# Scores of two 64-node graphs as 64 by 64 products in the two halves of the partitions, in place of masked 128 by 128 products

## The reference, cut to what matters

```python
h = relu(layernorm(x))
q, k, v = h @ Wq.T, h @ Wk.T, h @ Wv.T            # float32
rel = einsum('bnd,bmd->bnm', q, k) * adj.T         # 64 x 64 for each set
rel = rel / norm(rel, axis=2)
x = x + einsum('bnm,bmd->bnd', rel, v)
h = relu(layernorm(x))
for _ in range(3):                                 # w3, w4, w5, u3, u5: 256-wide layers
    a = adj @ h                                    # both halves of the input are the same
    z = sigmoid(a, h);  r = sigmoid(a, h);  c = tanh(a, r * h)
    h = (1 - z) * h + z * c
x = x + h
```

## Time and profile before

| | |
|---|---|
| median of three runs | 916.28 us (915.57 to 917.47) |
| the profiled execution | 915.86 us |
| its span, first to last instruction | 914.1 us |
| granted TensorE clock, mean | 0.996 of full speed |
| instructions | 14622 |
| busy | PE 98%, weight load 85%, DVE 83%, ACT 57%, GpSimd 12% |
| DMA | 98.73 MB, mean 108 GB/s |

### The profile page before, as it was taken

The page is one execution under the profiler, slowest core; times in us unless marked ns, Lnnn a source line. Parts: engine busy times, 40 slices in busy tenths (PEclk is TensorE's granted clock), DMA queues, the critical chain, the costliest instruction groups (busy, mean ns, idle before and its releaser), DMA issues.

```text
span 914.1 us, 14622 instructions
## 1 busy us (share of the span) xinstructions
PE 899.9 (98%) x4760; PEld 772.9 (85%) x4760; DVE 754.1 (83%) x1513; ACT 520.9 (57%) x892; POOL 107.8 (12%) x161
## 2 busy tenths in 40 slices
PE   8999999999999999999999999999999999999996
PEld 7878888888888888888888888888888888888885
DVE  5877879889788887888978888888879888797665
ACT  5465664656457574665745656456655556555552
POOL 1210102101021010210101101120101201020000
PEclk9999999999999999999999999999999999999999
DMA  6013222623245142441414513154221632224222
GB/s 180 24 50 113 93 93 94 205 69 110 84 125 186 46 138 86 143 161 46 147 60 138 184 69 115 46 163 158 91 92 53 204 110 92 92 102 129 73 66 92
DMA packets 75394, 98.73 MB, mean 108 GB/s; under 512 B 8176, under 2 KB 65776, under 8 KB 75376
## 3 DMA queue, kind: packets, MB, share of 16 engines
q1 hardware_dynamic: 75376, 98.50, 33.0%
HBM read 50.76 MB, written 47.71 MB: 108 GB/s over the span
## 4 chain that ended last, share of the span: by engine, by line
PE 95%; DVE 2%; issue 1%; DMA 1%; ACT 1%; SPq 0%; DVEq 0%
PE gate L410 14%; PE gate L411 14%; PE gate L412 14%; PE cand L412 9%; PE cand L410 9%; PE cand L411 9%; PE fea L552 9%; PE fea L485 3%; PE tok L410 3%; PE tok L411 2%; PE tok L412 2%; PE fea L410 1%; PE fea L412 1%; PE fea L411 1%; DMA x_s<-x 1%
## 5 line engine op out<-in xcount | busy, mean ns | idle before, releaser
L796 ACT ACTIVATE r_s<-gate,b_r 128x512 f32<-128x512 f32 x96 | 65.7, 690 | 126.5 <-PE gate L412 126.5
L1110 DVE TENSOR_TENSOR rh<-r_s,h 128x512 f32<-128x512 f32 x96 | 68.5, 745 | 31.1 <-ACT r_s L796 30.6
L809 ACT ACTIVATE z_s<-gate,b_z 128x512 f32<-128x512 f32 x96 | 64.1, 683 | 51.5 <-PE gate L412 51.5
L712 ACT ACTIVATE h_hi<-h 128x512 fp32r<-128x512 f32 x92 | 56.8, 628 | 39.9 <-DVE h L909 21.9
L1082 DVE SCALAR_TENSOR_TENSOR d_s<-z_s,h 128x512 f32<-128x512 f32 x96 | 63.4, 685 | 18.7 <-ACT z_s L809 18.7
L410 PE MATMUL gate<-h_hi,W_hi_u 128*128 128x512 f32 x192 | 77.9, 406 | 0.2 <-DVE h_lo L909 0.2
L815 ACT ACTIVATE c_s<-cand,b_c 128x512 f32<-128x512 f32 x96 | 64.3, 686 | 23.7 <-PE cand L412 22.4
L355 POOL TENSOR_TENSOR rstd<-vare,minus_half 128x4 f32<-128x4 f32 x32 | 42.0, 1312 | 298.8 <-DVE vare L943 298.8
L410 PE MATMUL gate<-a_hi,W_hi_w 128*128 128x512 f32 x192 | 75.6, 394 | 1.1 <-DVE a_lo L909 1.1
L410 PE MATMUL cand<-rh_hi,W_hi_u 128*128 128x512 f32 x192 | 76.3, 397 | 0.0
L411 PE MATMUL gate<-h_lo,W_hi_u 128*128 128x512 f32 x192 | 75.1, 391 | 0.0
(11 more groups left out here) (147 smaller groups left out, 2220.6 us busy)
## 6 DMA issues: line engine op xcount, KB each, us to landing
h_back<-h_trip SPq DMA_DIRECT2D x216, 128.0 KB, 2.8
h_trip<-h_turned SPq DMA_DIRECT2D x40, 512.0 KB, 2.6
out<-o_s SPq DMA_DIRECT2D x16, 512.0 KB, 4.0
x_s<-x SPq DMA_DIRECT2D x15, 512.0 KB, 4.9
hx_trip<-hx SPq DMA_DIRECT2D x14, 512.0 KB, 3.4
hx_back<-hx_trip SPq DMA_DIRECT2D x56, 128.0 KB, 2.8
h_trip<-h_blk SPq DMA_DIRECT2D x14, 512.0 KB, 3.0
h_trip_last<-h_turned SPq DMA_DIRECT2D x7, 512.0 KB, 3.5
```

What stands on the lines that cost most here:

```text
L712: return nc.scalar.activation(dst, src, ACT.Copy)
L796: nc.scalar.activation(r_s[:, c, :], gate[:, c, :], ACT.Sigmoid, bias=b_r[:, c:c + 1]).then_inc(r_ready, 1)
L809: nc.scalar.activation(z_s[:, c, :], gate[:, c, :], ACT.Sigmoid, bias=b_z[:, c:c + 1]).then_inc(z_ready, 1)
L1110: nc.vector.tensor_tensor(rh[:, c, :], r_s[:, c, :], h[s][:, c, :], ALU.mult).then_inc(rh_ready, 1)
```

## The change

TensorE's part in the rounds is done by a new `scores_by_set`: the two sets e = 0, 1 of a pair get a product of 64 weights by 64 moving columns each, still over all 128 features of a half c. The first lands in partitions 0 to 63 and columns 0 to 63 of the square, the second in partitions 64 to 127 and columns 64 to 127, so that the two off-diagonal squares aren't written. VectorE's part is done by `mask_by_set`, two operations of 64 partitions by 4 x 64 elements that read and write the diagonal squares alone. The other squares of S keep the zeros that the start's `mask_scores` wrote. The start is left as it was, and so are `fea`'s release, the order of all else and the semaphores' counts.

```diff
--- before.py
+++ after.py
@@ -486,6 +486,18 @@
                                                 start=c == 0, stop=c == C - 1)
                 last.then_inc(fea_full, 2)
 
+            def scores_by_set(n, n_q):
+                pe.wait_ge(fea_taken, 2 * n_q + 2)
+                fea_wait(n, 0)
+                fea_wait(n, 1)
+                for q in range(Q):
+                    for c in range(C):
+                        for e in range(2):
+                            nodes = slice(q * P + e * N, q * P + (e + 1) * N)
+                            last = nc.tensor.matmul(feaS[half(e), q, half(e)], hxT[:, c, nodes], q_s[:, c, nodes],
+                                                    start=c == 0, stop=c == C - 1)
+                last.then_inc(fea_full, 2)
+
             def norm_products(dst):
                 for b in range(HQ):
                     two = sq[:, 2 * b:2 * b + 2, :].rearrange("p q n -> p (q n)")
@@ -634,11 +646,11 @@
                 if attention and k == 2:
                     queries(2 * i + 2, use("q X"))
                     values(2 * i + 2, use("v X"))
-                    scores(use("rel X"), use("q X"))
+                    scores_by_set(use("rel X"), use("q X"))
                 elif attention and k == 4:
                     queries(2 * i + 3, use("q Y"))
                     values(2 * i + 3, use("v Y"))
-                    scores(use("rel Y"), use("q Y"))
+                    scores_by_set(use("rel Y"), use("q Y"))
                 candidate_rh(w, s)
                 if k == 5:
                     if new:
@@ -982,6 +994,13 @@
                 fea_wait(n, 1)
                 nc.vector.tensor_tensor(S[:], feaS, mask[:], ALU.mult).then_inc(fea_taken, 2)
 
+            def mask_by_set(n):
+                fea_wait(n, 1)
+                for e in range(2):
+                    last = nc.vector.tensor_tensor(S[half(e), :, half(e)], feaS[half(e), :, half(e)],
+                                                   mask[half(e), :, half(e)], ALU.mult)
+                last.then_inc(fea_taken, 2)
+
             def split_S(g):
                 dve.wait_ge(S_hi_ready, g + 1)
                 sub(S_lo[:], S[:], S_hi[:]).then_inc(S_lo_ready, 1)
@@ -1147,7 +1166,7 @@
                         take_q(use("q X"))
                         statistics(0, 2 * i + 3, 1, i + 2)
                         split_v(2 * i + 2, use("v X"))
-                        mask_scores(use("rel X"))
+                        mask_by_set(use("rel X"))
                         split_S(2 * i + 2)
                         sum_squares(2 * i + 2)
                         shifts(0, 2 * i + 3)
@@ -1174,7 +1193,7 @@
                     if attention:
                         take_q(use("q Y"))
                         split_v(2 * i + 3, use("v Y"))
-                        mask_scores(use("rel Y"))
+                        mask_by_set(use("rel Y"))
                         split_S(2 * i + 3)
                         sum_squares(2 * i + 3)
                 elif k == 5:
```

## The result

The changed kernel takes 909.28 us, the median of six runs (907.36 to 909.91), against 915.92 us of the kernel before in the same series (914.62 to 917.47). The ratio is 0.9921 with a 95% interval of 0.991 to 0.9932: 6.6 us faster, where 6.7 us slower was forecast. The profiled execution took 907.36 us and is the fastest of the six.

What follows compares the result with a forecast made beforehand. TensorE was taken to bound the kernel; 14 blocks x (0.08 us for the products + 0.40 us for the switches) = +6.7 us on 915.9, giving 922.6 us. The range was 904 to 928 us, the forecast's own 917.7 to 924.6.

Steps and rivals of the forecast that it cites:

- What bounds the kernel: Seven rounds: TensorE runs without a gap and waits for nothing, so a change in the scores goes straight into the time.
- The price of one record: Scores on TensorE: 111.9 ns per record now; 58.5 ns with load and stream halved and the fixed 5.2 ns kept.
- The new products: Scores of a block: 32 records one behind the other, 1.87 us against 1.79, +0.08 us a block.
- lower bound: New products: records of the two halves run side by side, 16 x 58.5 = 0.94 us, -0.85 us a block.
- The nearest row: Load of 128 weights in 107 to 110 ns, read as one weight per half-speed clock; used to choose the middle price.
- Entering and leaving: TensorE going to 64-wide outputs and back, twice a block: 0.2 us each, 0.40 a block, bounds 0 and 0.54.
- full restart: Upper bound at each width change: restart from empty, 0.27 us, twice a block 0.54 us.
- The sum: Whole kernel: 14 x (0.08 + 0.40) = +6.7 us, giving 922.6 us.
- Rival 1: Scores: the halves run side by side, -0.85 us a block before switches, 904.0 to 911.6 us; chance 0.30.
- VectorE: Mask as two operations of about 425 ns, +0.16 to +0.26 us a block, hidden by 2.1 and 1.3 us of cover.
- The signs to look for: Profile if right: records stepping 55 to 62 ns, scores 2.2 to 2.3 us a block, no PE wait, round 111.2 us.
- The hole on entering and leaving: First and last of a block's score records: a hole of 0.15 to 0.3 us, seen as a much longer matmul record.

Runs made afterwards that it cites:

- the kernel with doubled switches: The changed kernel with a block's scores cut in two by the last quarter of the values' products: 916.9 us, ratio 1.0007 to the kernel before.

## Why the prediction was wrong, point by point
**What bounds the kernel: right.** PE fills the rounds before and after, and what the scores gained went into the time. That "nothing is waited for" was read from a view that can't see short waits: the starts show 0.6 us of them for a_lo in the last rounds, too little to change the sum.

**The price of one record: right.** 58.5 ns was forecast and 58.4 measured, with the products in one half. The reading that a load of 128 weights alone paces a record was right too; with 128 weights and 64 columns it is 112 ns.

**The new products: wrong, and this is the step that failed.** The prediction took +0.08 us a block since "a load seems to begin only when the matmul ahead of it begins" and the loads would "stay one behind the other". That was read from a stream in which every product writes all 128 partitions. Such rows say nothing of two products that write different halves. Nor do they keep loads apart altogether: the four load records of the earlier trace rows, 0.19 us each, lie within 0.52 us. The runs show that loads and matmuls of the two halves both run side by side: 16 x 58.4 = 0.93 us, which is the lower bound that the prediction gave (0.94 us) and set aside; -0.85 us a block in place of +0.08, 13 us over the 14 blocks. The nearest row was near in its size and far in its kind. Bounds so far apart, of which no row showed the mechanism, deserved chances closer to each other than 0.30 against 0.42.

The page TensorEngine Tiling (Array Packing) of the Trainium skill has tiles run loads and matmuls in parallel (section Key Properties) and gives up to twice for a dimension of 64 (section Theoretical Speedup). The runs agree: 0.93 us against 1.86, when the switches are left out. With the switches it is 1.28 against 1.79, 1.4 times.

**Entering and leaving: right in size.** 0.40 us taken, 0.33 to 0.35 measured three times, inside the bounds of 0 and 0.54. The Trainium skill's page TensorEngine Tiling (Array Packing), section Key Properties, says that a change of tiling mode drains the engine; the prediction's full restart would be 0.54 us. The measured price is smaller, 0.35 us for both ways together. The trace shows a pause at each change of width, as by that rule, but it can't show a drain: the ends of matmul records are modelled, and the first load of the new width starts at 89.54 us, 0.07 us ahead of the end that the last wide record shows (89.33 + 0.28).

**The sum.** 14 x (-0.85 + 0.35) = -7.0 us, against -7.4 us counted in the trace and -6.6 us between the medians. Rival 1 was priced at 904.0 to 911.6 us and holds the result.

**VectorE: right.** 425 ns was forecast for one of the two mask operations and 416 measured. In the changed kernel's timeline, against the earlier trace rows:

```profile
90.95 0.85 DVE L1000 TENSOR_TENSOR S<-fea,mask 64x256 f32<-64x256 f32 x2
...
92.50 0.69 DVE L921 TENSOR_TENSOR S_lo<-S,S_hi 128x512 fp32r<-128x512 f32 x1 [0.70 <-ACT S_hi L724]
...
95.15 0.19 PEld L410 LDWEIGHTS tok<-v_hi,S_hi 128*128 128x128 f32 x1
...
97.71 0.69 DVE L921 TENSOR_TENSOR a_lo<-fea,a_hi 128x512 fp32r<-128x512 f32 x1
...
98.94 0.65 DVE L921 TENSOR_TENSOR a_lo<-fea,a_hi 128x512 fp32r<-128x512 f32 x1
...
99.44 0.39 PE L410 MATMUL gate<-a_hi,W_hi_w 128*128 128x512 f32 x1
```

S is ready 0.85 us after the mask's start instead of 0.69. S_lo is ready at 93.19 and wanted at 95.15, 2.0 us of cover; the first a_lo is ready at 98.40 and wanted at 99.44, 1.0 us where it was 1.3. Either mask gives the same time. The cover is thinner than the prediction took it, which read it in the first round: in the last rounds of the kernel before it is gone at three places, and the kernel with doubled switches shows what follows when more is taken.

**The signs to look for.** A step near 30 ns was named as rival 1's, and it is there as 58 ns a pair. The hole on entering and leaving is there too, in the starts (209 ns for 120, 107 for 58, and 0.21 us behind the last), but not as records much longer than their neighbours: the first two show 270 ns where the others show 222. A round of 111.2 us was forecast; it is 109.1.

## What to carry to other kernels
All of this was measured with full float32 products over 128 features. Two products of 64 weights that write different halves of the partitions run at the same time, loads included, if they stand within about three records of each other; written into the same half, or far apart in the program, they cost as much as one product of double the size and slightly more. Halving only the columns or only the weights buys nothing here, since load and stream each set a floor. A change of width costs some 0.35 us there and back, so small products belong together in one stretch, and that stretch must be worth more than this.

## What was not expected of the hardware
- Two matmuls of different halves start 6 to 7 ns apart, and their weight loads too, over the same 128 rows. The page TensorE: Matmul & The Clock Gate of the Trainium skill, Part 3 (Packing small matmuls), lets loads overlap matmuls in flight only where the row group differs; here both products take in all 128 rows, only the half of the partitions that they write differs, and loads start with the other half's matmul in flight. The measurement decides.
- A record of the free half is started ahead of up to three earlier ones that wait for the busy half: with groups of 4 records a block's starts span 0.98 us (0.93 when the sets alternate), with groups of 16 they span 1.68, with one half alone 1.86.
- Even where the scores wrote one half of the partitions only, for 2.2 us a block, the granted clock stayed at its upper level, 2.4 GHz: 0.996 in the mean, as in the kernel before.
